# The first layer of the small routed slots in plain float32, from a weight buffer and a transposed-row buffer of their own

## What is computed

```python
    gate_logits = jnp.einsum('bsd,ed->bse', x, gate_w) + gate_b + expert_bias
    top_idx = jnp.argmax(gate_logits, axis=-1)
    for e in range(NUM_EXPERTS):
        mask = (top_idx == e)[..., None].astype(x.dtype)
        h = jax.nn.relu(jnp.einsum('bsd,df->bsf', x, w1[e]) + b1[e])
        y = jnp.einsum('bsf,fd->bsd', h, w2[e]) + b2[e]
        out = out + mask * y
```

## Time and profile before

| | before |
|---|---|
| median of 3 runs | 1065.47 us (1065.38 to 1067.77) |
| profiled execution | 1066.7 us, span 1064.7 us |
| PE busy | 1039.9 us (98% of the span) |
| DVE, ACT, POOL busy | 773.6, 638.7, 373.1 us |
| mean granted TensorE clock | 0.994 of full |

### The profile page before, as it was taken

How to read it: one execution, slowest core, us unless ns; L and a number is a source line. 1 busy time by engine, 2 the same in 40 slices (tenths; PEclk the granted TensorE clock), 3 DMA queues, 4 the chain that set the end, 5 groups by cost and what they waited for, 6 DMA issues and landing times. The chain is left out here.

```text
span 1064.7 us, 20417 instructions
## 1 busy us (share of the span) xinstructions
PE 1039.9 (98%) x6692; PEld 933.5 (88%) x6692; DVE 773.6 (73%) x1281; ACT 638.7 (60%) x1152; POOL 373.1 (35%) x309
## 2 busy tenths in 40 slices
PE   6999999999999999999999999899999999999996
PEld 5998888989889898888877888899999999988885
DVE  5865657556575565758689889887778787588888
ACT  4554444444444444445574656789888989566664
POOL 3344443444434344453471782000000000164451
PEclk9999999999999999999999999999999999999998
DMA  5215111010111101203236366588787877332224
GB/s 178 73 56 198 41 40 59 26 73 0 39 59 39 59 0 59 79 1 139 66 115 257 109 221 233 160 250 268 241 262 241 268 247 247 126 119 99 108 70 138
DMA packets 72683, 134.73 MB, mean 127 GB/s; under 512 B 10048, under 2 KB 42688, under 8 KB 71616
## 3 DMA queue, kind: packets, MB, share of 16 engines
q1 hardware_dynamic: 63280, 120.65, 33.8%
q0 software_dynamic: 3072, 8.39, 2.4%
q10 hardware_dynamic: 6288, 5.16, 1.4%
HBM read 98.72 MB, written 35.45 MB: 126 GB/s over the span
## 5 line engine op out<-in xcount | busy, mean ns | idle before, releaser
L712 POOL TENSOR_TENSOR acc<-acc,ytmp 128x512 f32<-128x512 f32 x120 | 156.7, 1306 | 248.2 <-ACT ytmp L800 234.8
L1387 ACT ACTIVATE act_o<-ps,scan_bias 128x512 f32<-128x512 f32 x192 | 129.8, 688 | 103.5 <-PE ps L374 86.9
L865 DVE SCALAR_TENSOR_TENSOR hT_l<-ps,hT_h 128x512 fp32r<-128x512 f32 x128 | 87.8, 686 | 117.0 <-ACT hT_h L763 116.9
L800 ACT ACTIVATE ytmp<-ps,sel 128x256 f32<-128x256 f32 x256 | 107.6, 472 | 100.5 <-PE ps L1015 99.9
L372 PE MATMUL ps<-x1T,WB_h 128*128 128x512 f32 (+1 forms) x384 | 152.7, 398 | 2.3 <-DMA x1T<-xT_d 2.3
L374 PE MATMUL ps<-x1T,WB_l 128*128 128x512 f32 (+1 forms) x384 | 151.4, 394 | 0.0
L373 PE MATMUL ps<-x1T,WB_h 128*128 128x512 f32 (+1 forms) x384 | 150.1, 391 | 0.0
L1013 PE MATMUL ps<-vals_h,hT_h 128*128 128x256 f32 x512 | 145.2, 284 | 0.4 <-DVE hT_l L865 0.4
L1014 PE MATMUL ps<-vals_l,hT_h 128*128 128x256 f32 x512 | 143.6, 281 | 0.0
L1015 PE MATMUL ps<-vals_h,hT_l 128*128 128x256 f32 x512 | 143.4, 280 | 0.0
L763 ACT ACTIVATE hT_h<-ps 128x512 fp32r<-128x512 f32 x128 | 76.5, 598 | 99.6 <-PE ps L374 99.5
(11 more groups left out here) (220 smaller groups left out, 2647.1 us busy)
## 6 DMA issues: line engine op xcount, KB each, us to landing
raw<-w SPq DMA_DIRECT2D x92, 512.0 KB, 4.9
x1T<-xT_d SPq DMA_DIRECT2D x16, 512.0 KB
comb_b<-comb_d SPq DMA_DIRECT2D x8, 1024.0 KB
xs_d<-zeros ACTq DMA_DIRECT2D x1, 4992.0 KB, 18.8
x_in<-x SPq DMA_DIRECT2D x8, 512.0 KB, 3.8
x_d<-x SPq DMA_DIRECT2D x8, 512.0 KB, 4.2
xn_d<-xn SPq DMA_DIRECT2D x8, 512.0 KB, 2.6
xT_d<-nT_h SPq DMA_DIRECT2D x8, 512.0 KB, 2.6
```

The costliest lines, as they stand in the source:

```text
L712: pool.tensor_tensor(dst[:, 2:4, :], acc[:, 2:4, :], ytmp[:, k % 2, :, :], ALU.add).then_inc(acc23, 1)
L800: act.activation(ytmp[:, k % 2, j - 2, :], yb(k, j), ACT.Copy, scale=sel[:, j, k:k + 1]).then_inc(y_23, 1)
L865: dve.scalar_tensor_tensor(out=hT_l[:, k % 2, :], in0=ps[:, k % 2, :], scalar=0.0, in1=hT_h[:, k % 2, :].bitcast(F32), op0=ALU.max, op1=AL ...
L1387: act.activation(act_o[:, i % 2, w, :], ps[:, 3 * (i % 2) + w, :], func, bias=scan_bias[:, w, i:i + 1]).then_inc(act_g, 1)
```

## The change

The small slots (k=2) no longer use raw1, w1_h, w1_l, sT_h and sT_l. Their w1 is loaded as it is into a new buffer `w1_small`, and ACT copies their transposed rows unrounded into `sT_small`. The first layer is 16 plain float32 matmuls instead of 48 in float32r. The second layer of small slots stays in three parts.

raw1 and its parts now go from big slot to big slot. `bigs(r, k)` counts the big slots before (r, k). In slot k=0 the split is for k=1, in k=1 for k=0 of the next round, in k=2 there is none. SP loads raw1 at k=0 and k=1 for the big slot after next; raw2 for n+2 is another expert's then, and has a slot_e load of its own. At the end of k=0 SP also loads w1_small for k=2 of this round. The buffer x1T moves to the end of the memory to make room.

```diff
-    x1T = nc.alloc_sbuf_tensor_at("x1T", [P, 2, 2, DC, GT], F32R, offset=end_a - 8 * KB)
+    at_x1T = nc.sbuf_usable_end // 32 * 32 - 16 * KB
+    x1T = nc.alloc_sbuf_tensor_at("x1T", [P, 2, 2, DC, GT], F32R, offset=at_x1T)
...
+    sT_small = rc("sT_small", [P, DC, P], F32)
...
+    w1_small = rc("w1_small", [P, DC, F1], F32)
...
+    def bigs(r, k):
+
+        return ST * (r + k // ROUND) + min(k % ROUND, ST)
...
-            def raw1_half(n, h, e):
-                if not zero(n):
-                    wait_alone(sp, w1_lo, 2 * (n - 1) + h + 1)
+            def raw1_half(nb, h, e):
+                if not zero(nb):
+                    wait_alone(sp, w1_lo, 2 * (nb - 1) + h + 1)
...
+            def load_w1_small(r):
+                if not zero(r):
+                    wait_alone(sp, l1_full, FJ // 2 * ROUND * r)
+                e = expert(ROUND * r + ST)
+                for h in (0, 1):
+                    sp.dma_start(w1_small[:, :, h * HALF1:(h + 1) * HALF1],
+                                 a["w1"][bass.ds(e, 1), h].rearrange("a p c f -> p (a c) f")).then_inc(w1s_in, 16)
...
+                if not small(k) and bigs_left(r, k) > 1:
+                    e = expert(n + ROUND)
+                    raw1_half(bigs(r, k) + ST, 0, e)
+                    raw1_half(bigs(r, k) + ST, 1, e)
                 if left(r, k) > 1:
-                    e = expert(n + 2)
-                    raw1_half(n + 2, 0, e)
-                    raw1_half(n + 2, 1, e)
-                    raw2_half(n + 2, 0, e)
+                    raw2_half(n + 2, 0, expert(n + 2))
+                if k == 0 and left(r, k) > 1:
+                    load_w1_small(r)
...
-                        pe.wait_ge(w1_lo, 2 * n + 1 + q // 2)
+                        if small(k):
+                            pe.wait_ge(w1s_in, 32 * (r + 1))
+                        else:
+                            pe.wait_ge(w1_lo, 2 * bigs(r, k) + 1 + q // 2)
...
+                            if small(k):
+                                last_mm = pe.matmul(ps[:, q, (j % 2) * W:(j % 2 + 1) * W], w1_small[:, c, f],
+                                                    sT_small[:, c, :], start=c == 0, stop=c == DC - 1)
+                                continue
...
+                if small(k):
+                    act.activation(sT_small[:], turned, ACT.Copy).then_inc(sT_ok, 1)
+                else:
+                    act.activation(sT_h[:], turned, ACT.Copy).then_inc(sT_hi, 1)
...
-                    if q == 1 and left(r, k) > 0:
-                        w1_half(n + 1, 0)
+                    if q == 1 and not small(k) and bigs_left(r, k) > 0:
+                        w1_half(bigs(r, k) + 1, n, 0)
...
-                    rows_lo(r, k + 1)
-                    w1_half(n + 1, 1)
+                    if not small(k + 1):
+                        rows_lo(r, k + 1)
+                    if not small(k) and bigs_left(r, k) > 0:
+                        w1_half(bigs(r, k) + 1, 1)
```

More of the change, by code:

```diff
@@ L229, in build @@
     sef = rr("sef", [P, N_ROUND * ROUND], F32)
-    assert rr.at - at_raw <= 16 * KB and end_a + 8 * KB <= nc.sbuf_usable_end
-    assert rc.at <= end_a - 8 * KB and max(rb.at, at_raw + 16 * KB) <= at_post
+    assert rr.at - at_raw <= 16 * KB and end_a <= at_x1T + 8 * KB
+    assert rc.at <= at_x1T and max(rb.at, at_raw + 16 * KB) <= at_post
     ps = nc.alloc_psum_tensor("ps", [P, 8, 512], F32)
@@ L579, in build @@
     scat = [sem(f"scat{b}") for b in range(XN_RING)]
-    b1_in, b2_in, rows_in = (sem(n) for n in ("b1_in", "b2_in", "rows_in"))
+    b1_in, b2_in, rows_in, w1s_in = (sem(n) for n in ("b1_in", "b2_in", "rows_in", "w1s_in"))
     r1_in, r2_in = [sem(f"r1_in{h}") for h in (0, 1)], [sem(f"r2_in{h}") for h in (0, 1)]
@@ L605, in blocks, with small, bigs_left @@
         return (4 * r + ST * k, ST) if k < ST else (T // P + r, 1)
+    def bigs(r, k):
+        return ST * (r + k // ROUND) + min(k % ROUND, ST)
+    def small(k):
+        return k % ROUND == ST
+    def bigs_left(r, k):
+        return N_BIG - 1 - bigs(r, k) if isinstance(r, int) else N_BIG
     def every_slot(slot, eng):
@@ L1398, in split_late, with w1_half @@
                 act.activation(chunks[name][2], staged(name), ACT.Copy).then_inc(wb_hi, 1)
[L1400 to L1403, removed]
+            def w1_half(nb, n, h):
+                act.wait_ge(r1_in[h], 16 * (nb + 1))
+                if not zero(nb):
+                    act.wait_ge(l1_full, FJ // 2 * n + 2 * (h + 1))
                 f = slice(h * HALF1, (h + 1) * HALF1)
@@ L1416, in rows_hi @@
                 act.wait_ge(T_full, n + 1)
-                act.activation(sT_h[:, :, 0:st * P], ps[:, 6, 0:DC * st * P].rearrange("p (c t) -> p c t", c=DC),
-                               ACT.Copy).then_inc(sT_hi, 1)
+                turned = ps[:, 6, 0:DC * st * P].rearrange("p (c t) -> p c t", c=DC)
+                if small(k):
+                    act.activation(sT_small[:], turned, ACT.Copy).then_inc(sT_ok, 1)
+                else:
+                    act.activation(sT_h[:], turned, ACT.Copy).then_inc(sT_hi, 1)
             def relu(n, q, W):
@@ L1443, in slot @@
                     round_e(n, q, st * P)
-                    if q == 1 and left(r, k) > 0:
-                        w1_half(n + 1, 0)
+                    if q == 1 and not small(k) and bigs_left(r, k) > 0:
+                        w1_half(bigs(r, k) + 1, n, 0)
                 if left(r, k) > 0:
                     rows_hi(r, k + 1)
-                    w1_half(n + 1, 1)
+                    if not small(k) and bigs_left(r, k) > 0:
+                        w1_half(bigs(r, k) + 1, n, 1)
                     w2_half(n + 1, 0)
@@ L1469, in _ @@
                     if g == B_FIRST - 1 and i in (4, 6):
-                        w1_half(0, (i - 4) // 2)
+                        w1_half(0, 0, (i - 4) // 2)
                     if g == B_FIRST - 1 and i == MC - 3:
@@ L1697, in total, with w1_half @@
                     dve.tensor_tensor(x1_b[:], side4, x1_b[:], ALU.add).then_inc(fin_ok, 1)
-            def w1_half(s, h):
-                dve.wait_ge(w1_hi, 2 * s + h + 1)
+            def w1_half(nb, h):
+                dve.wait_ge(w1_hi, 2 * nb + h + 1)
                 f = slice(h * HALF1, (h + 1) * HALF1)
@@ L1704, in rows_lo @@
             def rows_lo(r, k):
[L1705 to L1708, removed]
+                dve.wait_ge(sT_hi, bigs(r, k) + 1)
+                dve.tensor_tensor(sT_l[:], ps[:, 6, :].rearrange("p (c t) -> p c t", c=DC), sT_h[:].bitcast(F32),
+                                  ALU.subtract).then_inc(sT_ok, 1)
             def w2_half(s, h):
@@ L1747, in slot @@
                     low_e(n, q, st * P)
-                    if q == 1 and left(r, k) > 0:
-                        w1_half(n + 1, 0)
+                    if q == 1 and not small(k) and bigs_left(r, k) > 0:
+                        w1_half(bigs(r, k) + 1, 0)
                 if left(r, k) > 0:
-                    rows_lo(r, k + 1)
-                    w1_half(n + 1, 1)
+                    if not small(k + 1):
+                        rows_lo(r, k + 1)
+                    if not small(k) and bigs_left(r, k) > 0:
+                        w1_half(bigs(r, k) + 1, 1)
                     w2_half(n + 1, 0)
```

## The result

The changed kernel takes 1069.04 us (median of 18 runs, 1067.82 to 1071.53) against 1065.73 us for the kernel before (18 runs). The ratio is 1.0031, with a 95% interval from 1.0024 to 1.0037: slower by 0.3%, where the prediction had 1057.3 us and 1061.5 as its upper end. The profiled execution has a span of 1066.7 us, against 1064.7.

The account below looks back on a forecast made before the run. PE was taken to bound the kernel; 1.91 us saved a round less a 0.6 stall left 1.3, 7.8 over six rounds, plus 0.4 in round 0: 8.2 us off the 1065.47 median, 1057.3 us, range 1052.0 to 1061.5.

Parts of the forecast that it names:

- (d): Rival for small slots' first layer: passes set the cost, 7.1 us against 5.31, total 1078 us; chance 0.01.
- (e): Rival: granted clock falls while PE runs float32 or stalls, costing up to 24 us, total over 1065; chance 0.02.
- (b): Rival: small slot's raw2 transfer takes 5.5 to 6.6 us and eats the gain, about 1065; sign: rounds of 31+; chance 0.08.
- Term 1: PE, small slots' first layer: 32 records of 106 ns, 3.40 us instead of 5.31; saves 1.91 a slot, 13.4 for seven.
- Term 3: Big slot behind a small one: raw2's second half, landing 4.6 us after issue, delays relu; 0.5 us lost per round.
- Term 4: New SP loads at the end of k=0 delay the small slot's raw2 by 2.1 us; with Term 3, S is 0.6.
- S: PE's stall per round from late raw2 transfers: 0.5 to 0.8 us, taken as 0.6.
- the slack of 0.41: Small slot: how late, in us, ACT's first split may be before PE waits in its second layer.
- S is half of it: Small slot: a later PE waits less, so the stall counts on both sides and halves to 0.3 to 0.8 us.
- A stall here also covers that of term 3: A small-slot stall also absorbs the next big slot's 0.5 us; both together 0.5 to 0.8 us a round.
- Round 0: First round, with the ranking on DVE: 1.91 won less 0.76 and 0.74 lost, a gain of 0.4 us.
- At nothing: moving x1T: Moving x1T to a new place in memory costs nothing, since no instruction changes.

Follow-up runs that it names:

- e4: The changed kernel with w1_small loaded in round 0 alone, all small slots using that expert's first layer: 1063.10 us, ratio 0.9969 to the kernel before.
- e3: The changed kernel with w1_small loaded a round early, at the end of k=2 for the next round: 1064.37 us, ratio 0.9975 to the kernel before.
- e12: The changed kernel with w1_small transfers carrying only 32 of 512 columns from round 1 on: 1063.97 us, ratio 0.9984 to the kernel before.
- e1: The kernel before with only x1T moved to the changed kernel's place, 1664 bytes higher: 1068.36 us, ratio 1.0014 to the kernel before.
- e5: e3 with raw2's second half split after the second first-layer quarter in k=0 slots, except round 0: 1069.03 us, ratio 1.0024 to the kernel before.

## Why the prediction was wrong, by its own steps

- **Where to look was right:** PE is freed, its feeders decide. The records (32), ACT's waits for raw2 in the two slots named, PE's short stalls on eT_l at L1393, the full clock (1.00 in all slot windows) and no wait for w1_small came as written. Rivals (d) and (e) didn't happen. Rounds of 31 and more, the sign given for (b), did.
- **Term 1 was a little large.** 106 ns a record came from a stretch of 16 that ends at a change of operation; the 32 in the small slot take 111.6. The slot wins 1.78 us with all, not 1.91: 12.5 instead of 13.4 us.
- **Term 3's mechanism was right, its size too small.** "I use 4.6": the landing was taken from one row. In the changed kernel ACT takes this half 4.4 to 5.8 us after its issue, 5.1 on the mean of seven, and the issue is 5.1, not 4.54, into the slot. In e4 the big slots behind small ones lose 0.85 us a round over the same six rounds; the term said 0.5.
- **Term 4 failed,** and it is the step that decides: S measured 1.8 over rounds 1 to 6 (10.8 us in sum) where 0.6 was taken. Most of it is size. "I add 2.1 us" measured 2.5 (9.37 - 6.89), and the small slot's half, taken at 4.6 to 5.6 us, is taken by ACT 5.2 to 6.3 after its issue (mean 5.6). With the measured means the term's own count gives 5.11 + 5.14 + 0.97 + 16.86 + 5.56 = 33.6 us where it had 31.0 to 32.0. ACT wants that half at 30.2 + S; less the slack of 0.41 the stall is 3.0 - S, and half of that is 1.5. The rest, 0.3 us, is "S is half of it". The reasoning took the late transfer as fixed in time and PE as coming later to it. In fact SP's queue behind it moves along, with the next raw2 and by relu the next round: a loop of 31.9 us on the mean, which waiting doesn't shorten. "A stall here also covers that of term 3" fell by the same: the big slots lost 2.9 of the 10.8. e3 and e12 give back 0.8 of S by moving or thinning the load.
- **Round 0** lost 1.95 us instead of 1.50.
- **"At nothing: moving x1T"** was wrong: 2.1 us in the profiled span behind the slots, 1.7 by the medians (e1). No instruction changes, but 1152 of them take 4 ns longer.
- **The sum again,** for the profiled span: 12.5 won on PE, less 10.8, 1.95 and 2.1, plus 0.4 that the first slot ended earlier (683.85, 684.25), which is chance: -2.0, which is 1066.7 - 1064.7. Against the forecast gain of 8.2 that is a miss of 10.2 us: about 7.2 by S, 2.1 by x1T, 0.9 by term 1 and 0.45 by round 0, less that 0.4. Rival (b) named late transfers of raw2 and had nearly the price of the slots; it had no loop, and with x1T on top the result lies beyond it. (Its "from 5.5 on the total gain is under 3.2 us" is off by a little: a landing of 5.5 leaves 0.4 + 6 x 0.5 = 3.5.)

## What to carry to other kernels

When a change shortens the engine that bounds a loop, add up the loop that doesn't run through that engine (issue, landing, conversion, back to the same issue) by the rows: where it is longer than that engine's own round, its length is the new round, and waiting doesn't shorten it. Take landings from many rows and not from one. Put a new large load behind the transfers that are awaited next, not ahead of them, and look at what each freed wait was hiding, here b1's single buffer (e5). A buffer that moves should be priced like an edit: compare the distances between the matmuls that read it.

## What was not expected of the hardware

The start-to-start time of a 512-column matmul depended on the byte address of its moving operand, 229 ns or 233 ns, by its remainder of 256 (96 or 224) in five places; other remainders weren't tried, and three of the places have one profile each. The length in the records is 0.39 in both cases. And the plain float32 matmul of 128 columns costs two records of 111.6 ns, the same as one float32r matmul of 128 columns each (111 ns), at a granted clock of 1.00. So at this width three float32r matmuls (333 ns) are dearer than one in float32 (223 ns). The Trainium skill ("TensorE: Matmul & The Clock Gate", section "Wait — 56ns, not 53.3ns?") gives 55.6 ns for 128 columns and 215.7 for 512 back to back on a warm array; this trace, where each matmul also loads its weights, shows about twice that at 128 and 229 to 233 at 512. What holds the narrow ones at 111 ns no run here shows.
